# Leaf stage in groups of four tiles, twelve weight buffers, a third of the weight copies on VectorE

## The reference

```python
def _fff(x, node_w, node_b, w1, b1, w2, b2):
    cur = jnp.zeros((N,), jnp.int32)
    for _ in range(DEPTH):
        score = jnp.einsum('nd,nd->n', xf, node_w[cur]) + node_b[cur]
        cur = 2 * cur + 1 + (score >= 0).astype(jnp.int32)
    sel = jax.nn.one_hot(cur - N_NODES, N_LEAVES, dtype=xf.dtype)
    hidden_all = jax.nn.relu(jnp.einsum('nd,ldh->lnh', xf, w1) + b1[:, None, :])
    hidden = hidden_all * sel.T[:, :, None]
    return jnp.einsum('lnh,lho->no', hidden, w2) + sel @ b2
q, k, v = _fff(xn, *q_params), _fff(xn, *k_params), _fff(xn, *v_params)
attn = jax.nn.softmax(jnp.einsum('bqd,bkd->bqk', q, k) / 16, axis=-1)
return x + attention(xn) + jnp.einsum('bqk,bkd->bqd', attn, v)
```

## Time and profile before

| | us |
|---|---|
| median of 3 runs | 3935.44 (3934.48 to 3940.17) |
| the profiled execution, its own time | 3935.01 |
| its span, first to last instruction | 3933.2 |
| mean granted TensorE clock | 0.981 |

### The profile page before, as it was taken

How to read it: one execution, slowest core, us unless ns; L and a number is a source line. 1 busy time by engine, 2 the same in 40 slices (tenths; PEclk the granted TensorE clock), 3 DMA queues, 4 the chain that set the end, 5 groups by cost and what they waited for, 6 DMA issues and landing times. The chain is left out here.

```text
span 3933.2 us, 63904 instructions
## 1 busy us (share of the span) xinstructions
PE 3720.3 (95%) x23714; PEld 1464.6 (37%) x23714; DVE 3152.2 (80%) x5433; ACT 2786.4 (71%) x3257; POOL 1550.2 (39%) x2057
## 2 busy tenths in 40 slices
PE   7997999999999999999999999999999879899999
PEld 5664222222222222222222222222222245588888
DVE  6776899999989999998999999899999433345454
ACT  4343888888888888887888788888888946522221
POOL 2320353263235325333532543253344357763330
PEclk9998999999999999999999999999999989899999
DMA  8775111111111111111101111110112069732220
GB/s 298 269 265 186 33 39 42 50 33 34 58 33 39 34 57 33 34 52 34 44 28 52 39 39 33 47 49 28 44 38 83 33 237 327 231 118 87 74 86 22
DMA packets 224553, 330.85 MB, mean 84 GB/s; under 512 B 29281, under 2 KB 165092, under 8 KB 219636
## 3 DMA queue, kind: packets, MB, share of 16 engines
q1 hardware_dynamic: 205812, 276.40, 21.3%
q0 software_dynamic: 18432, 50.36, 3.8%
HBM read 169.27 MB, written 156.34 MB: 83 GB/s over the span
## 5 line engine op out<-in xcount | busy, mean ns | idle before, releaser
L1734 DVE TENSOR_REDUCE first_rows<-psum 128x1 f32<-128x512 f32 x4000 | 2509.4, 684 | 173.1 <-PE psum L185 157.5
L1579 ACT ACTIVATE arena<-psum,exp_scale 128x1024 f32<-128x1024 f32 x2048 | 2159.8, 1111 | 275.8 <-PE psum L1439 269.8
L1455 PE MATMUL psum<-arena 128*32 128x512 f32 x8200 | 1107.5, 612 | 1.2 <-ACT arena L1579 0.6
L1619 POOL TENSOR_TENSOR arena<-arena 128x16 f32<-128x16 f32 x129 | 376.9, 2922 | 1504.0 <-ACT arena L1545 1504.0
L185 PE MATMUL psum<-arena 48*128 48x512 f16 x2048 | 649.6, 391 | 51.1 <-DVE first_rows L1734 22.8
L185 PE MATMUL psum<-first_rows 48*128 48x512 f16 x2048 | 622.7, 386 | 36.7 <-ACT arena L1539 7.7
L185 PEld LDWEIGHTS psum<-arena 48*128 48x128 f16 x2048 | 157.8, 93 | 865.2 <-DVE first_rows L1734 721.1
L185 PEld LDWEIGHTS psum<-first_rows 48*128 48x128 f16 x2048 | 154.9, 92 | 836.8 <-DVE first_rows L1734 715.1
L1439 PE MATMUL psum<-arena 50*128 50x512 f16 x2048 | 444.8, 382 | 11.6 <-ACT arena L1579 8.5
L1439 PE MATMUL psum<-first_rows 50*128 50x512 f16 x2048 | 447.3, 384 | 6.9 <-DMA first_rows<-arena 3.0
L1136 ACT ACTIVATE mix_arena<-psum,mix_arena 128x1024 f32<-128x1024 f32 x64 | 71.4, 1115 | 327.1 <-DVE mix_arena L1156 327.1
(11 more groups left out here) (186 smaller groups left out, 3944.0 us busy)
## 6 DMA issues: line engine op xcount, KB each, us to landing
scratch_split<-route_arena SPq DMA_DIRECT2D x64, 512.0 KB, 3.2
scratch_sorted_x<-route_arena SPq DMA_DIRECT2D x60, 512.0 KB, 4.7
scratch_sorted_y<-leaf_arena SPq DMA_DIRECT2D x60, 512.0 KB, 3.9
first_rows<-scratch_split SPq DMA_DIRECT2D x384, 64.0 KB, 2.2
arena<-scratch_split SPq DMA_DIRECT2D x384, 64.0 KB, 2.2
leaf_arena<-scratch_sorted_x SPq DMA_DIRECT2D x44, 512.0 KB, 5.8
leaf_start<-in_leafw SPq DMA_DIRECT2D x2, 5128.0 KB, 17.6
arena<-in_x SPq DMA_DIRECT2D x18, 512.0 KB, 4.9
```

Source lines behind the costliest of these rows:

```text
L1455: last = nc.tensor.matmul(value_bank[32 * j:32 * j + 32, :], vaug[:, batch % 2, kt, 2 * pair + j % 2, :], prob[:, step % 2, j, :], start=k ...
L1579: nc.scalar.activation(prob[:, step % 2, 2 * h:2 * h + 2, :], score[:, 2 * h:2 * h + 2, :], ACT.Exp, scale=exp_scale[:, s % 2, s // 2:s // ...
L1619: nc.gpsimd.tensor_tensor(linv[:, c], total, minus_one, ALU.pow).then_inc(ochain, 1)
L1734: nc.vector.tensor_reduce(halfmax[:, odd, 2 * m + h, qt, c:c + 1], aux_bank[bank], AX.X, ALU.max).then_inc(bank_used[bank], 1)
```

## The change

TensorE's loop goes over groups of four tiles in place of pairs: eight transposes into two banks, the hidden matmuls of four tiles into one bank, the outputs of four tiles into two banks; signals of hidden and output come once per group. `WBUF` is 12. Each third tile's weights (n % 3 == 2) are copied by VectorE: behind the addition of tile n it waits for that addition, loads the leaf number of tile n+12 and copies. GpSimd copies the others. Waits for weights look at two counters. `yg` moves into the memory `first_rows` of the attention stage, which is free by then.

```diff
-WBUF = 8
+WBUF = 12
...
-    yg = ar.take(YBUF, GROUP_T, DIM)
-    xT = ar.take(2, 2, KC, P)
-    hT = ar.take(2, P)
+    yg = Arena(first.tensor).take(YBUF, GROUP_T, DIM)
+    xT = ar.take(2, GROUP_T, KC, P)
+    hT = ar.take(2, 2, P)
...
+    dve_tiles = [0]
+    for n in range(TILES_ALL):
+        dve_tiles.append(dve_tiles[-1] + (n % 3 == 2))
+
+    def wait_weights(eng, n):
+
+        eng.wait_ge(wsel_pool, n - dve_tiles[n])
+        eng.wait_ge(wsel_dve, dve_tiles[n])
...
-                    sp.wait_ge(wsel_ready, TILES_F)
+                    wait_weights(sp, TILES_F)
...
+            def turn(g):
+                pe.wait_ge(xg_in[g % XBUF], 16 * (g // XBUF + 1))
+                for j in range(2):
+                    if g >= 1:
+                        pe.wait_ge(xT_ready, 2 * (g - 1) + j + 1)
+                    for n in range(2):
+                        for k in range(KC):
+                            last = nc.tensor.transpose(bank(j)[:, (KC * n + k) * P:(KC * n + k + 1) * P],
+                                                       xg[g % XBUF][:, 2 * j + n, k * P:(k + 1) * P], ident)
+                    last.then_inc(xT_full, 1)
+
+            def hidden(g):
+                pe.wait_ge(xT_ready, 2 * g + 2)
+                wait_weights(pe, GROUP_T * (g + 1))
+                if g >= 2:
+                    pe.wait_ge(hid_ready, GROUP_T * (g - 1))
+                for j in range(2):
...
+                last.then_inc(hid_full, 1)
+
+            def outputs(g):
+                pe.wait_ge(hid_ready, GROUP_T * (g + 1))
+                if g >= 2:
+                    pe.wait_ge(y_ready, GROUP_T * (g - 1))
+                for j in range(2):
                     for n in range(2):
...
+            for g in range(GROUPS + 2):
+                if g < GROUPS:
+                    turn(g)
+                if 0 <= g - 1 < GROUPS:
+                    hidden(g - 1)
+                if g >= 2:
+                    outputs(g - 2)
...
-                choose(n)
-                if n == first:
+                if n % 3 < 2:
+                    choose(n)
+                if n == early:
...
         def _(dve):
+            def choose(n):
+
+                if n % TILES_F <= 2:
+                    dve.wait_ge(leafw_in[n // TILES_F], 16)
+                leaf = dve.value_load(tablei[0:1, n:n + 1], min_val=0, max_val=LEAVES - 1)
+                nc.vector.tensor_copy(wsel[:, n % WBUF], leafw[n // TILES_F % 2][:, bass.ds(leaf, 1)].rearrange("p a n -> p (a n)")
+                                      ).then_inc(wsel_dve, 1)
+
+            dve.wait_ge(start.table_in, 16)
+            for n in range(2, WBUF, 3):
+                choose(n)
             for n in range(TILES_ALL):
                 g = n // GROUP_T
-                dve.wait_ge(y_full, n // 2 + 1)
+                dve.wait_ge(y_full, g + 1)
...
+                if n + WBUF < TILES_ALL and (n + WBUF) % 3 == 2:
+                    dve.wait_ge(y_ready, n + 1)
+                    choose(n + WBUF)
```

More of the change, by code:

```diff
@@ L806, in gather, with leaf_stage @@
                                ).then_inc(self.gathered[f][b % 2], 16)
-def leaf_stage(nc, ctx, ps, w, scratch, start, mix):
+def leaf_stage(nc, ctx, ps, w, scratch, start, mix, first):
     ar = Arena(ctx.enter_context(nc.sbuf_tensor("leaf_arena", [P, LEAF_WORDS], F32)))
@@ L896, in out_pair @@
-            def out_pair(p):
-                pe.wait_ge(hid_ready, 2 * p + 2)
-                if p >= 2:
-                    pe.wait_ge(y_ready, 2 * (p - 1))
-                for n in range(2):
-                    last = nc.tensor.matmul(bank(4 + 2 * (p % 2) + n)[:, 0:DIM], hT[half(n), p % 2],
-                                            wsel[half(n), (2 * p + n) % WBUF, W2], start=True, stop=True)
+            def turn(g):
[8 more added lines that the diff above has]
+                    last.then_inc(xT_full, 1)
@@ new lines, in hidden @@
+            def hidden(g):
[4 more added lines that the diff above has]
+                for j in range(2):
+                    for k in range(KC):
+                        for n in range(2):
+                            last = nc.tensor.matmul(bank(2 + g % 2)[half(n), j * P:(j + 1) * P],
+                                                    wsel[:, (GROUP_T * g + 2 * j + n) % WBUF, k * LEAF_W:(k + 1) * LEAF_W],
+                                                    xT[:, g % 2, 2 * j + n, k], start=k == 0, stop=k == KC - 1,
+                                                    tile_position=(0, LEAF_W * n))
+                last.then_inc(hid_full, 1)
@@ new lines, in outputs @@
+            def outputs(g):
[3 more added lines that the diff above has]
+                for j in range(2):
+                    for n in range(2):
+                        last = nc.tensor.matmul(bank(4 + 2 * (g % 2) + n)[:, j * DIM:(j + 1) * DIM], hT[half(n), g % 2, j],
+                                                wsel[half(n), (GROUP_T * g + 2 * j + n) % WBUF, W2], start=True, stop=True)
@@ L932, in _, with relu @@
-            relu(PAIRS - 1)
+            def relu(g):
+                act.wait_ge(hid_full, g + 1)
+                if g >= 2:
+                    act.wait_ge(y_full, g - 1)
+                for j in range(2):
+                    for n in range(2):
+                        nc.scalar.activation(hT[half(n), g % 2, j], bank(2 + g % 2)[half(n), j * P:(j + 1) * P], ACT.Relu,
+                                             bias=wsel[half(n), (GROUP_T * g + 2 * j + n) % WBUF, REC - 1:REC]
+                                             ).then_inc(hid_ready, 1)
@@ L934, in _ @@
+            for g in range(GROUPS):
+                if g >= 2:
+                    act.wait_ge(hid_full, g - 1)
+                for j in range(2):
+                    act.wait_ge(xT_full, 2 * g + j + 1)
+                    nc.scalar.activation(xT[:, g % 2, 2 * j:2 * j + 2].rearrange("p n k t -> p (n k t)"), bank(j), ACT.Copy
+                                         ).then_inc(xT_ready, 1)
+                if g >= 1:
+                    relu(g - 1)
+            relu(GROUPS - 1)
         @block.gpsimd
```

65 lines of the change are left out of this document (11 added, 54 removed).

## The result

The changed kernel takes 3941.73 us (median of 20 runs, 3935.33 to 3952.53), the kernel before in runs beside it 3934.74 (median of 20, 3928.06 to 3941.65). The ratio is 1.0019 with a 95% interval of 1.0012 to 1.0027. That is 7.0 us more, where the prediction had added up +3 (3938 on 3935). It lies under the 0.2% that the prediction had named as the least that counts as slower, though with 20 runs of each kernel the interval leaves out 1. The profiled execution took 3942.24 us with a span of 3940.4, 7.2 us more than before.

What follows compares the result with a forecast made beforehand. TensorE was taken to bound the leaf stage before, the twelve-buffer ring after. On 3935 us: pace +2, gathers -4, fill +2, collisions +3 gave 3938 us, no change; own range 3928 to 3943, with rivals 3914 to 3960.

Steps and rivals of the forecast that it cites:

- the ring of twelve buffers: Ordinary leaf-stage groups: hidden matmuls wait for buffers freed late, 3.65 us per group, 0.47 of it TensorE waiting; chance 0.38.
- three kinds of group: VectorE's copy behind the third addition, the second, or the first and fourth: releases of 5.66, 5.20 and 4.66 us.
- collisions: GpSimd and VectorE copying at once in the leaf stage: 0.06 us per group, +3 us in all.
- VectorE's register load and arithmetic: Before each VectorE weight copy: wait for the addition, leaf number load; 0.80 us taken, bounds 0.68 and 0.84.
- GpSimd's answer: In the ring's release: GpSimd's copy starts 0.85 us after the addition that frees its buffer.
- rival 2: GpSimd's and VectorE's copies shut each other out: copies over 1 us, groups 4 us apart, 3957 us; chance 0.22.
- fill: Start of the leaf stage: first outputs come behind five phases of four tiles; +2 us (1 to 3).
- gathers: GpSimd's 16 tiles there keep 16 gathers but only 11 copies: 26 us for 30, so -4 us.
- stalls: Two stalls of some three groups each behind the 5 MB weight loads; they hang on these and stay.
- A clock drop is no term: From 3373 to 3390 us TensorE was busy 9.2 of 17 us and the clock stayed at 1.00; nothing added.
- rival 1: The ring does not bind: pace falls towards TensorE's 3.18 us per group, 3919 us named; chance 0.30.
- Rival 3: VectorE's weight copy runs one element per cycle, 0.76 us in place of 0.50: +12 us, 3947 us; chance 0.10.

Runs made afterwards that it cites:

- e2: The changed kernel with sixteen weight buffers in place of twelve; ratio 0.9975 to the kernel before, pace 3.46 and 3.50 us per group.
- e5: The changed kernel with VectorE copying a fixed leaf's record, without its register load; ratio 0.9949 to the kernel before.
- e1: The changed kernel (groups of four, twelve buffers) with all weight copies back on GpSimd; ratio 0.9992 to the kernel before.
- e3: The kernel before, in pairs, with twelve weight buffers for eight and yg moved, all copies on GpSimd; ratio 0.9982 to the kernel before.
- e4: The kernel before, in pairs with eight buffers, with every third weight copy on VectorE; ratio 1.0011 to the kernel before.
- e9: The changed kernel with rows loaded for the first eight groups only; ratio 1.0019 to the kernel before.
- e11: Groups of four, all copies on GpSimd, loads ahead of the wait, 8 of 256 columns of later rows; ratio 0.9974 to the kernel before.
- e7: The changed kernel with leaf numbers loaded ahead of their use on both VectorE and GpSimd; ratio 0.9950 to the kernel before.
- e10: Groups of four, all copies on GpSimd, loads ahead of the wait, rows for the first eight groups only; ratio 0.9966 to the kernel before.

## Why the prediction was right, and where it was lucky

That the change is worth nothing was right, the size less so (+7.0 us for +3), and the step that carried it was right too: **the ring of twelve buffers sets the pace, not TensorE.** TensorE's waits end with a weight copy, as shown above. The releases were forecast at 5.66, 5.20 and 4.66 us for the three kinds of group, 5.17 on average. In the first stretch they measured 5.24, 5.21 and 5.08, mean 5.18: the mean fits since the first kind was 0.42 too long and the third 0.42 too short, which is luck. The pace of 3.66 for 3.65 and TensorE's idle time of 0.48 us per group (5.6 us over 43/3.66 groups) for 0.47 follow from the same mean and confirm nothing more. Sixteen buffers (e2) make it faster, as they must. In the second stretch the releases are 6.38, 4.92 and 5.69, mean 5.67, and the pace is 3.92. All 47 ordinary steps together have 175.9/47 = 3.74 us, so pace and collisions, for which the sum had +5, measured +6.5.

Inside that sum several terms were off and offset each other:

- *TensorE's own pace*: 3.11 us (e5), not 3.18, near the lower bound of 3.09. A phase takes 1.02 to 1.07, as summed up.
- *VectorE's register load and arithmetic*: from the addition's end to the copy 0.76 us with a load of 0.30, for the 0.80 that I took. But the mean load is 0.44 and 0.55, and from addition to copy it is 0.95 and 1.03 us on average, beyond my upper end of 0.84. The row was there: the earlier trace rows has 1387 ns as the longest of 240 loads on GpSimd, beside the median of 287, and I took the median for all. In the kernel before, 56 of the 240 are over 0.6 us.
- *GpSimd's answer*: 0.85 us from the addition to the copy. I had read it from the pair's second addition. The buffer is free with the first, 0.42 long and ended at 3340.10, and the load behind it is one of the long ones, so the answer was 1.19 us. With a load of 0.29 us it is 0.71 (first of the two additions at 3320.06 until 3320.48, copy at 3321.19). My 0.85 happened to lie between. Nor did GpSimd idle 0.88 us for want of a buffer, as the prediction's first paragraph says: the buffer was free before the copy in front ended (3340.41), and the idle time is that load and the arithmetic behind it. The load in the kernel before:

```profile
L940 POOLq TENSOR_LOAD <-leaf_start x1: 756/756/756, 3340.1 to 3340.1; - x1
```

- *VectorE's copy*: 0.494 us alone, for the 0.50 taken, right.
- *Collisions*: they are real, as rival 2 had them: a copy of VectorE that starts while GpSimd's runs takes up to 1.05 us and ends about 0.35 us after it, and one of GpSimd that starts while VectorE's runs ends about 0.58 after it. I had added 0.06 us per group; VectorE's copies lose 0.16 on average, four in three groups, so 0.2 per group in VectorE's time alone. Rival 2's sign, copies over 1 us, is there, and the second stretch with 3.92 is nearer to its 4.0 us per group than to the forecast; the first is not, and the time stays under its 3957. In the second stretch one of VectorE's copies in four is shut out for long.

The Trainium skill had this rule, and I gave it to a rival: SBUF — State Buffer, section "Who interferes with whom". The trace agrees with it (0.50 alone, 1.04 behind a copy of GpSimd; without VectorE's copies none of GpSimd's over 0.726 in e1).

Of the *remaining terms* the fill came out, and the gathers did (26.1 us for 26), though not only for the reason I gave: twelve buffers alone, with all 16 copies on GpSimd, save 5.1 us (e3) where the change saves 4.1, and a third of the copies on VectorE in pairs saves 3.8 (e4). In groups of four with all copies on GpSimd only 1.5 are saved (e1, 37.5 us); that GpSimd has no time left there to fill the ring is likely, not shown. The *stalls* were the step that failed: "hang on the weight loads and stay" was right for the first and missed +3.1 us at the second. All eight kernels in groups of four that load every row take 18.7 to 22.7 us there, and the three in pairs 15.8 to 17.5, so it belongs to the grouping. What the term lacked is TensorE's wait of 8.33 us for rows and the clock of 0.50 behind it, 10.25 us long for 7.00. In e9 to e11, which leave the later rows out wholly or nearly, the same steps take 15.9 to 17.5 us, which points to the rows' transfers beside the weight load. At the first load TensorE waits longer for rows too (4.30 us for 1.69), and yet the three steps take no longer; why stays open.

*A clock drop is no term* was read from a stretch between two drops. The kernel before, at the gathers:

```profile
3366.25:3373.00 6.75, 6.15 (x31) 3.42 (x27) 1.51 (x4) 2.05 (x5) 6.23 (x8) 0.50 0.70 231
...
3390.00:3397.00 7.00, 6.39 (x35) 3.85 (x32) 1.75 (x6) 2.65 (x6) 4.83 (x8) 0.51 0.60 191
```

Between the first and the last addition the clock is at 0.50 for some 27.5 us in the kernel before and 31.0 in the changed one, most of the difference at the second weight load. The term was small, but not nothing.

The *rivals*: rival 1's reasoning is borne out by e5 and e7, but only if the load is taken out of the way; the changed kernel itself leaves it behind the wait, as the argument against it said. Rival 3 is refuted: its copy would take 0.76 us alone, the row has 0.494, which against 0.260 for the cast of 192 elements makes 0.52 ns for each further one.

## What to carry to other kernels

Take a register load off the path between the event that frees a buffer and the copy that fills it: load the number before the wait. Here this turned a change worth nothing (1.0019) into the fastest kernel (0.9950), by two edits that add no instruction. When a row gives minimum, median and maximum, ask where the maxima sit before the median goes into a sum; and try a longer ring by itself first, since twelve buffers in the old kernel (0.9982) did more than the whole change.

## What the runs showed of the hardware that I had not expected

- A register load from SBUF takes 0.28 us on GpSimd and 0.30 on VectorE, but 0.56 to 1.25 us nearly always when it begins 0.4 to 1.6 us behind the issue of a 512 KB store of y: 26 of 27 such loads in e10 and 11 of 12 in the changed kernel, but none of the 54 in e10 that began over 2 us behind it. That the store is the cause was not isolated.
- A VectorE copy that overlaps GpSimd's is stretched from 0.49 to as much as 1.05 us, and GpSimd's from 0.72 to mostly 0.96 to 1.05, with both in SBUF and one source each.
- An addition of one pointer operand over 641 elements takes 0.554 us, 0.06 more than the bare copy; the 0.408 us for 256 elements with two pointer operands don't carry over.
